# Graph convolution and mixture of experts on one core: where layer 2's dense table units and linear layers stand

## What is computed

```python
h   = layernorm(x)
deg = segment_sum(w, dst) + 1;  dinv = rsqrt(deg)
out = relu(gcn(h, W1, b1));  out = gcn(out, W2, b2)     # gcn: segment_sum((x @ W)[src] * dinv[src] * w * dinv[dst], dst)
                                                        #      with a self loop of weight 1 per node, + b
out = relu((out - mean(out, 0)) * rsqrt(var(out, 0) + 1e-5) * gamma + beta + h)
x   = x + out
f   = layernorm(x)
p   = softmax(f @ gate_w + gate_b);  the two largest of 8 experts per node
x   = x + sum over the two of p_e * (gelu(f @ W1_e + b1_e) @ W2_e + b2_e)
```

## Time and profile before

| | us |
|---|---|
| median of 3 runs | 2357.84 (2357.24 to 2361.3) |
| the profiled execution, its own time | 2363.68 |
| its span, first to last instruction | 2361.9 |
| PE busy | 1928.7 (82%) |
| POOL busy | 1650.7 (70%) |
| DVE busy | 933.1 (40%) |
| ACT busy | 423.6 (18%) |

### The profile page before, as it was taken

How to read it: one execution, slowest core, us unless ns; L and a number is a source line. 1 busy time by engine, 2 the same in 40 slices (tenths; PEclk the granted TensorE clock), 3 DMA queues, 4 the chain that set the end, 5 groups by cost and what they waited for, 6 DMA issues and landing times.

```text
span 2361.9 us, 30351 instructions
## 1 busy us (share of the span) xinstructions
PE 1928.7 (82%) x8786; PEld 1400.5 (59%) x8787; DVE 933.1 (40%) x2598; ACT 423.6 (18%) x1137; POOL 1650.7 (70%) x1651
## 2 busy tenths in 40 slices
PE   1044592999999997867999999999983838999998
PEld 1044351666566665644666666666652828999997
DVE  7999310222222234422223232333237793333332
ACT  1800100000000001100000000000004673444443
POOL 0777777777777777775777777777756556666675
PEclk6555796999999999977999999999986559999999
DMA  9994542666666654444666656665672246888895
GB/s 325 342 333 130 191 125 55 201 197 206 190 198 206 201 159 149 149 118 145 197 188 192 194 186 194 187 197 182 194 234 80 78 146 174 214 208 210 209 215 127
DMA packets 289701, 438.37 MB, mean 186 GB/s; under 512 B 41634, under 2 KB 225163, under 8 KB 289451
## 3 DMA queue, kind: packets, MB, share of 16 engines
q1 hardware_dynamic: 207979, 268.31, 34.9%
q0 software_dynamic: 79872, 166.48, 27.5%
q10 hardware_dynamic: 1728, 2.13, 0.3%
HBM read 341.71 MB, written 96.51 MB: 186 GB/s over the span
## 4 chain that ended last, share of the span: by engine, by line
POOL 54%; issue 18%; PE 16%; DVE 7%; DMA 3%; ACT 1%; SPq 0%; POOLq 0%; DVEq 0%; ACTq 0%
POOL arena L597 43%; POOL pair_weights L582 11%; PE psum L1724 7%; PE psum L1732 6%; DMA out_dram<-ACC 2%; PE psum L1715 1%; DVE edge_cols L1248 1%; DVE stats L1254 1%; DVE X L1251 1%; ACT ACC L816 1%; DVE ACC L1368 1%; DMA arena<-conv_rows,edge_cols 1%; PE psum L1674 0%; PE psum L1508 0%; DVE ACC L1243 0%
## 5 line engine op out<-in xcount | busy, mean ns | idle before, releaser
L597 POOL DMA_INDIRECT arena<-conv_rows,edge_cols x1064 | 1019.9, 959 | 340.7 <-issue 324.0
L1549 PE MATMUL psum<-arena,X 128*128 128x448 f32 x1960 | 821.5, 545 | 41.0 <-DMA arena<-pair_weights 28.0
L1599 PE MATMUL psum<-arena 128*128 128x256 f32 x2128 | 583.8, 391 | 113.4 <-DMA arena<-conv_rows,edge_cols 109.2
L1599 PEld LDWEIGHTS psum<-arena 128*128 128x128 f32 x2128 | 401.7, 195 | 333.1 <-issue 275.1
L1549 PEld LDWEIGHTS psum<-arena,X 128*128 128x128 f32 x1960 | 375.3, 192 | 267.2 <-issue 218.5
L1178 DVE TENSOR_TENSOR ACC<-ACC,psum 128x256 f32 x76 | 32.1, 422 | 910.4 <-PE psum L1567 910.4
L582 POOL DMA_INDIRECT pair_weights<-scale_b,mean_b x252 | 257.0, 1020 | 132.8 <-issue 76.5
L1157 DVE TENSOR_SCALAR arena<-iota,edge_cols 128x128 f32<-128x128 f32 x1064 | 281.2, 359 | 0.4 <-DVE ACC L1084 0.2
L663 POOL DMA_INDIRECT out_dram<-ACC x105 | 166.5, 1586 | 103.8 <-DMA out_dram<-ACC 86.5
L746 ACT ACTIVATE arena<-psum 128x256 f32<-128x256 f32 x76 | 29.0, 382 | 1033.4 <-PE psum L1599 1033.4
L1724 PE MATMUL psum<-ACC,arena 128*128 128x128 f32 x1680 | 205.7, 275 | 0.2 <-DVE ACC L1395 0.2
(11 more groups left out here) (307 smaller groups left out, 1375.1 us busy)
## 6 DMA issues: line engine op xcount, KB each, us to landing
arena<-pair_weights SPq DMA_DIRECT2D x469, 224.0 KB, 3.4
arena<-in_L_ffn_W_dram SPq DMA_DIRECT2D x113, 512.0 KB, 7.5
pair_weights<-zeros SPq DMA_DIRECT2D x5, 10976.0 KB, 73.1
arena<-conv_rows,edge_cols POOLq DMA_INDIRECT x1064, 2.9
conv_rows<-X SPq DMA_DIRECT2D x13, 896.0 KB, 5.9
X<-in_x_dram SPq DMA_DIRECT2D x12, 896.0 KB, 11.2
rows_for_experts<-ACC SPq DMA_DIRECT2D x7, 910.0 KB, 4.3
out_dram<-X SPq DMA_DIRECT2D x6, 896.0 KB
```

The source lines that it names most:

```text
L597: pool.indirect_dma_start(G[:, n * D:(n + 1) * D], None, y_tab[layer], bass.IndirectOffsetOnAxis(srcT[:, t:t + 1], 0)).then_inc(gathered[n ...
L1549: ins = m.matmul(bank(6 + c, BW), X[:, t * D + c * P:t * D + (c + 1) * P], table, start=(t == 0), stop=(t == NT - 1))
L1599: ins = m.matmul(bank(2 * (k % 2), D), S[:, n * P:(n + 1) * P], G[:, n * D:(n + 1) * D], start=(j == 0), stop=(j == GT - 1))
```

## The change

Three edits.

1. `BEFORE` for layer 2 goes from 0 to 8: eight units are done ahead of group 0, and the counts of all groups but the last three stay as they are; the last three have 1, 0 and 0. The blocks end in groups 6, 13, 20, 27 and 35.
2. `LINEARS` for layer 2 goes from 3 to 4, and a group in which the last block ends no longer counts as one where a block ends. The groups 6 to 37 take 1, 0, 4, 1, 1, 0, 1, 1, 4, 1, 1, 1, 1, 0, 1, 4, 1, 1, 1, 1, 1, 0, 4, 1, 1, 1, 1, 1, 1, 0, 4, 4 linears, and the rest has 4 tiles.
3. The out-of-bounds row numbers move from a tile of their own to column 1 of `flag_i`, and the iota that writes them moves from POOL's first instructions to just ahead of the four scatters that use them, with a wait for itself.

```diff
@@
         bad, bad2, flag_i = sb("bad", 4), sb("bad2", 4), sb("flag_i", 4, I32)
+        no_row = flag_i[:, 1:2]
@@
-        no_row = sb("no_row", 1, I32)
@@
-        BEFORE, EARLY = (49, 0), 21
+        BEFORE, EARLY = (49, 8), 21
@@
-        LINEARS, LINEAR_STEP = (6, 3), (2, 3)
+        LINEARS, LINEAR_STEP = (6, 4), (2, 3)
@@
-                most = 1 if layer == 1 and n == 0 else 2 if k in ends else LINEARS[layer]
+                most = 1 if layer == 1 and n == 0 else 2 if k in ends[:NB - 1] else LINEARS[layer]
@@
-                g.iota(no_row[:, :], [[0, 1]], base=NP + P, channel_multiplier=1)
@@
+                chain(g.iota(no_row, [[0, 1]], base=NP + P, channel_multiplier=1))
                 for u in range(4):
-                    pool.indirect_dma_start(out, bass.IndirectOffsetOnAxis(no_row[:, 0:1], 0), zeros[:, :], None,
+                    pool.indirect_dma_start(out, bass.IndirectOffsetOnAxis(no_row, 0), zeros[:, :], None,
```

## The result

The changed kernel takes **2338.28 us** (median of 4 runs, 2336.97 to 2340.6) against 2358.91 (4 runs, 2357.24 to 2361.3) for the kernel before in the same comparison: ratio 0.9916, 95% interval 0.9901 to 0.993, a gain of 20.6 us. The forecast was 2348.4 with a range of 2344.5 to 2356.5. The sign was right, the size was wrong by a factor of two, and the time lies outside the range.

A forecast was written before the change was run, and what follows sets the result against it. POOL's gathers were taken to set layer 2's time, with PE nearly as loaded. Landing -4.6, linears -4.8 and iota 0 made -9.4 us off the median 2357.84: 2348.4 us, range 2344.5 to 2356.5.

The forecast's parts named there:

- part 3: POOL's head: moving the row-number iota late costs 0, hidden by POOL's 2.10 us wait; without cover 0 to 0.95 us.
- Parts 1 and 2, -9.4: Layer 2: moved units free the last landing (-4.6 us), four fewer left-over linears behind it (-4.8 us).
- The units in front cost nothing: Start of layer 2: eight units ahead of group 0 delay PE, but slack stays positive, so POOL never stalls; cost 0.
- Slack(0): Start of group 2's first gather less group 0's sum copy, PE's lead over POOL: 2.9 us forecast.
- slack(31): Start of group 33's first gather less group 31's sum copy: 2.0 us forecast, positive so POOL does not wait.
- The rival of a stall, small or large: Layer 2, POOL waits for PE: slow clock, +13 us, chance 0.06; small stalls lose 3 to 8 us, chance 0.16.
- The dear block end moves to group 6: PE in layer 2: the block end costing 5.7 us (wait 4.0, clock 1.7) falls in group 6, before in group 29.
- Landing, -4.6: Tail: X load ends before the last gather, which lands in 2.9 us, not 7.49; bounds 0 and -4.9.
- Four fewer linears, -4.8: Tail: four fewer left-over linears at 1.19 us of DVE each; bounds -3.9 (slow clock) and -6.4 (never slow).
- Code behind the load: PE's jump before L1647: code waits until the second weights' load drains, leaving 4.6 us gain; chance 0.16, shared with landing missing.

The follow-up runs named there:

- The late X load: Changed kernel with SP holding the load of X back until group 36 has been added: 2342.86 us, against 2338.11 for the changed kernel.
- second profile: The changed kernel itself run once more, nothing changed, beside three others on one chip: 2338.11 us, ratio 0.9908 to the kernel before.
- flag tile alone: Kernel before with row numbers in column 1 of flag_i, the iota still among POOL's first instructions: 2359.64 us, ratio 0.9999.
- `tile_at` late: Kernel before with the float iota of tile_at made late, the int32 iota left at the head: 2363.26 us (before 2362.45).
- the three kernels of the table's last row: Kernel before, iota late, unread int32 iota between scatters and gathers: 2349.93 us; kernel before, rows by late tensor_copy: 2351.95; changed kernel, five linears a group: 2336.15.

## Why the prediction was wrong

**The failed step is part 3, "Cost 0".** I priced the iota by its own 0.1 us and by what covers it where it arrives. The cover held: POOL still waits 2.10 us for L1378 ahead of its first expert gather. What failed is the bound: I gave 0 to 0.95 us and nothing below zero, though I named no reason that excludes a gain. The edit removed an instruction from the head of the engine that sets the time for 43% and 11% of the span, and 1316 DMAs stood behind it. The runs put -13.6 us in that place (0.9942, interval 9.9 to 17.7 us). By the medians of the durations, 7 ns for each of 1064 gathers and 9 ns for each of 252 scatters, it is 9.7 us; by the busy times it is 11.2 between the profiles of before and of the third edit alone (gathers 1019.9 to 1012.0, scatters 257.0 to 253.7) and 13.4 between those of before and after. What the runs gained beyond that is not located. The reading that would have warned me needs no foresight of the mechanism: with 1316 like instructions on the chain, 1 ns each is 1.3 us, so an edit to their stream cannot be bounded by its own duration.

**Parts 1 and 2, -9.4: right mechanism, measured -7.5** (0.9969, interval 4.7 to 10.1 us). Step by step:

- *The units in front cost nothing*: right. They took 13.7 us (forecast 15.5), because the clock came back after 3 us and not 6 to 7. Slack(0) was 5.9 and slack(31) 3.35, both over the forecast; POOL never waited for PE. The rival of a stall, small or large, falls. (From group 8 on the forecast's own slacks are 0.4 too low: 3.2 + 0.9 - 1.1 is 3.0 and not 2.6.)
- *The dear block end moves to group 6*: right. PE's waits for the block addition are 5.5 us in four, the longest 4.0 (7.1 and 4.0 before):

```profile
PE psum L1549 <- DVE ACC L1169: 5.5, 4, 4.0
```

- *Landing, -4.6*: the time from the last gather's issue to the rest fell by 3.7 in the two profiles. The late X load gives 4.75 back, so the mechanism is shown, though not its exact size. But the term is mis-sized: over all the kernels below it is -1.9. The last gather landed in 4.1 to 4.2 us and not in the 2.9 that I took, where with the old plan it took 6.8 at the median: 2.6 less. From its landing to the first left-over linear it then takes 3.4 to 3.5 us where it took 2.8, since something else is late next: the load slows gathers of group 37 instead, "whose products nobody waits for yet" was wrong, PE falls behind, and the four linears in that group, which I had put in free time of PE, lie on the chain.
- *Four fewer linears, -4.8*: 7.0 in the two profiles. In before the clock was 0.50 for the first 5.8 us of the rest, in after 1.00 all the time; -6.4 was my bound for never slow in after.
- *Both terms were read off an unlucky execution.* The profile of before has a tail of 27.6 us. Eleven kernels with the old units and linears had 21.7 to 25.4 (median 24.5), three with the new ones (after, its second profile, the first two edits alone) 16.9 to 17.6 (median 16.9). Split as above at the first left-over linear, the medians fell from 9.6 to 7.7 and from 14.5 to 9.2: -1.9 and -5.3. The medians of the whole tail differ by 7.6, which is what the runs say (7.5). The last gather's landing, 7.49 us in before, was 6.5 to 7.5 in the eleven (median 6.8), so it was unlucky by 0.7 only. More of the bad luck is the clock. From the first left-over linear to L1647 it took 12.5 to 12.9 us in the three of the eleven whose mean clock there was 0.99 or 1.00. Three such stretches (flag tile alone, `tile_at` late, before; the third number from the end is the clock):

```profile
1764.25:1777.00 12.75, 8.51 (x32) 5.52 (x32) 9.82 (x26) 5.65 (x13) 0.00 (x0) 1.00 1.10 336
...
1766.14:1781.71 15.57, 10.33 (x32) 7.35 (x33) 10.00 (x26) 6.77 (x15) 0.00 (x0) 0.83 1.06 325
...
1765.23:1781.40 16.17, 10.65 (x32) 7.77 (x32) 10.00 (x26) 6.78 (x15) 0.00 (x0) 0.71 0.92 288
```

  Less the gap ahead of L1647 (3.96, 5.08 and 5.40), the first is 8.8 us for eight linears; the three kernels of the new plan have 4.0 for four. So four linears at full clock are 4.8 us, as forecast. In before the clock added 2.0 (10.8 and not 8.8) and the gap 0.3 against after, which makes the 7.0.
- *Code behind the load*: falls. L1647 starts at 1754.75, behind a gap of 5.12 us (6.04 in the second profile, 5.40 in before), while the load of the second weights still fills the DMA engines (share 1.09 from 1754 to 1758). The gap did grow a little: it was 3.7 to 5.1 us in the eleven kernels of the old plan, at the median 4.6, and 5.1, 5.2 and 6.0 in the three of the new. The Trainium skill (DMA: Bandwidth & Descriptors, Queues, rings and completion order) says that a DMA engine takes turns between queues packet by packet; that PE went on before the load had drained agrees.

**What stays open** is why the int32 iota does it. Shown, but for the rival named above (the late instruction): it must run ahead of the first indirect DMA, a float one does not do it, two are as one, its output's address is no matter, and it touches scatters and layer gathers but not the expert stage's. The Trainium skill (GPSIMD Engine Reference, Instruction dispatch) says that POOL's instructions run as software routines that a resident dispatcher calls. A different routine or a different state left behind by it would fit, but that is a guess: no run here looks inside.

## What to carry to other kernels

Before an edit is priced, ask which engine's stream it touches: on the engine that issues over a thousand like instructions on the chain, compare the mean and the minimum duration of these between the two profiles first, and give an edit there a bound below zero as well. Try int32 iotas behind the first indirect DMA of GpSimd; that cost nothing here (all behind the tail took the same time to 0.1 us) and was worth 0.6%. Take terms of a tail from several profiles, not from one, where a single transfer or a clock step carries the term, and look at the granted clock of each first.

## What the hardware showed that I had not expected

- With one int32 iota of 128x1 (0.12 us) ahead of the first indirect DMA the later gathers take 953 ns and not 946, the scatters 967 and not 958 at the median, and those of the expert stage the same with it and without.
- The clock came back 3.0 us after PE's first work of layer 2 in after and 6.3 us after it in before, though PE worked without a gap in both.
- The first 27 scatters start every 1.38 us in before and every 1.26 in after; that is 27 x 0.10 (by the means, 1.41 and 1.31) = 2.8 of the scatters' 4.6 us. But these 2.8 us do not hang on the iota alone: the mean is 1.41 as well in the three kernels of the table's last row, which have none ahead, and 1.36 with the third edit alone.
- A gather beside the X load mostly takes 6 to 7.5 us to land (8.7 for the last one of the late X load), against 2.9 at the median of all.
